# Score weights of both batches in the prologue, and U on eight array tiles

## What is computed

```python
q, k, v = heads(layernorm(x) @ Wq), heads(ctx @ Wk), heads(ctx @ Wv)
attn = softmax(q @ k.T / 8)                       # per head, over 77
x = x + tanh(g_xattn) * (merge(attn @ v) @ Wo + bo)
h = relu(fixed_quant(qlinear(layernorm(x), w1, b1)))
x = x + tanh(g_ffn) * qlinear(h, w2, b2)          # qlinear rounds input, weight and bias
```

## Time and profile before

| | us |
|---|---|
| median of 3 runs | 125.9 (125.42 to 126.14) |
| the profiled execution | 125.8 |
| its span, first to last instruction | 123.8 |
| busy: PE / PEld / DVE / ACT / POOL | 118.5 / 107.4 / 98.2 / 78.2 / 84.6 |

### The profile page before, as it was taken

The page is one execution under the profiler, slowest core; times in us unless marked ns, Lnnn a source line. Parts: engine busy times, 40 slices in busy tenths (PEclk is TensorE's granted clock), DMA queues, the critical chain, the costliest instruction groups (busy, mean ns, idle before and its releaser), DMA issues.

```text
span 123.8 us, 2908 instructions
## 1 busy us (share of the span) xinstructions
PE 118.5 (96%) x1029; PEld 107.4 (87%) x1029; DVE 98.2 (79%) x218; ACT 78.2 (63%) x167; POOL 84.6 (68%) x157
## 2 busy tenths in 40 slices
PE   7999999979999999999999999999999999999990
PEld 2689968969995999999999999999999997988780
DVE  3017999698999989989899999999797969447981
ACT  4155591999888484999384857566664728357520
POOL 3002229288794979698989958995899595987610
PEclk9999999999999999999999999999999999999999
DMA  2999699300000000000002000100200020020104
GB/s 68 338 266 334 227 380 382 139 5 0 3 0 8 0 0 3 0 0 5 0 0 85 5 0 36 48 5 3 83 1 0 5 87 0 0 80 10 54 30 169
DMA packets 5311, 8.86 MB, mean 72 GB/s; under 512 B 1175, under 2 KB 2226, under 8 KB 5170
## 3 DMA queue, kind: packets, MB, share of 16 engines
q1 hardware_dynamic: 5210, 8.61, 19.5%
q10 hardware_dynamic: 88, 0.08, 0.2%
HBM read 6.59 MB, written 2.10 MB: 70 GB/s over the span
## 4 chain that ended last, share of the span: by engine, by line
PE 86%; DVE 5%; ACT 3%; POOL 2%; issue 2%; DVEq 0%; POOLq 0%; ACTq 0%
PE sc_ps L741 21%; PE of_ps L774 20%; PE h_ps L801 9%; PE tr_ps L753 7%; PE of_ps L816 7%; PE tr_ps L686 4%; PE of_ps L679 3%; PE h_ps L708 3%; PE tr_ps L724 2%; PE h_ps L695 2%; PE tr_ps L816 1%; PE sc_ps L816 1%; POOL probs L266 1%; PE sc_ps L695 1%; PE of_ps L782 1%
## 5 line engine op out<-in xcount | busy, mean ns | idle before, releaser
L741 PE MATMUL sc_ps<-a_sb,xT 128*128 128x308 f32 x192 | 31.2, 311 | 0.0
L774 PE MATMUL of_ps<-u_sb,pT 128*128 128x256 f32 x240 | 30.6, 279 | 0.3 <-ACT x2T L414 0.2
L774 PEld LDWEIGHTS of_ps<-u_sb,pT 128*128 128x128 f32 x240 | 29.1, 188 | 1.2 <-issue 1.1
L741 PEld LDWEIGHTS sc_ps<-a_sb,xT 128*128 128x128 f32 x192 | 27.5, 189 | 0.7 <-issue 0.4
L382 ACT ACTIVATE probs<-probs,rstd 128x616 f32<-128x616 f32 x16 | 13.1, 817 | 23.1 <-DVE probs L543 23.0
L408 ACT ACTIVATE hid_q<-h_ps,b1z 128x256 int8<-128x256 f32 x58 | 24.8, 495 | 3.9 <-PE h_ps L801 3.9
L266 POOL TENSOR_TENSOR probs<-probs,rden 128x616 f32<-128x616 f32 x16 | 19.5, 1221 | 3.2 <-DVE rden L553 3.2
L311 POOL CAST hid<-hid_q 128x512 bf16<-128x512 int8 x27 | 15.8, 611 | 2.0 <-ACT hid_q L408 2.0
L801 PE MATMUL h_ps<-x2T,w1T 128*128 128x256 bf16 x128 | 16.6, 273 | 0.0
L538 DVE TENSOR_REDUCE mx<-sc_ps 128x8 f32<-128x616 f32 x16 | 12.7, 792 | 4.7 <-PE sc_ps L741 4.6
L394 ACT CAST pT<-tr_ps 128x640 fp32r<-128x640 f32 x16 | 11.1, 691 | 4.8 <-PE tr_ps L753 4.8
(11 more groups left out here) (103 smaller groups left out, 187.7 us busy)
## 6 DMA issues: line engine op xcount, KB each, us to landing
w_sb<-in_L_ffn_w_dram SPq DMA_DIRECT2D x2, 1024.0 KB, 10.9
out_dram<-x_sb SPq DMA_DIRECT2D x7, 256.0 KB, 2.5
x_sb<-in_x_dram SPq DMA_DIRECT2D x4, 256.0 KB, 8.6
x_sb<-in_x_dram SPq DMA_DIRECT2D x1, 1024.0 KB, 9.8
wk_sb<-in_L_xattn_Wk_dram SPq DMA_DIRECT2D x1, 512.0 KB, 3.8
wq_sb<-in_L_xattn_Wq_dram SPq DMA_DIRECT2D x1, 512.0 KB, 5.7
wv_sb<-in_L_xattn_Wv_dram SPq DMA_DIRECT2D x1, 512.0 KB, 8.3
wo_sb<-in_L_xattn_Wo_dram SPq DMA_DIRECT2D x1, 512.0 KB, 8.5
```

What stands on the lines that cost most here:

```text
L741: ins = nc.tensor.matmul(sc_ps[:, a, 0:HALF], xT[:, T % 2, p, c, :], a_sb[:, q, T // TB, c, HALF * a:HALF * a + HALF], start=first, stop=last)
L774: ins = nc.tensor.matmul(attn_ps, pT[:, T % 2, p, P * c:P * c + P], u_sb[:, q, MC * (T // TB) + c, :], start=first, stop=last)
```

## The change

A is made for both batches at once: each matmul has 154 columns (77 of each batch) in place of 77, in four units (c, half) that go to four pairs of PSUM banks, all in the prologue. ACT copies batch 0's part as the high part and batch 1's part whole to `a1_whole`; POOL makes batch 1's high part (a cast) and low part out of that (`a1_parts`, once ahead of `rstd_first(2, 4)`, once in step 0). The two ACT copies in each of steps 0 and 1 go.

U is made with the even heads' values on rows 0 to 63 and the odd heads' on rows 64 to 127. Each matmul takes 64 rows and 32 columns; even and odd windows alternate, and the tables EVEN and ODD put four windows of each parity in a round, so that a round has eight different tiles. The heads' order in the probabilities becomes even heads first. A window that straddles two head pairs takes two matmuls: 24 for a batch in place of 20. Batch 1's U moves from step 3 to step 2. Its first two low parts are made on POOL (steps 2 and 3), one in place of DVE. In the loop, DVE takes `denominators(1)` first in step 0 and ACT takes the exponentials of tile 1 first; in the prologue ACT takes `exponentials(0)` ahead of `xT_copy(2)`. The values go to `vz` in one copy of 128 rows in place of two of 64 each time.

```diff
+EVEN = ((0, 0), (1, 0), (2, 0), (3, 1)), ((4, 1), (5, 2), (2, 1), (7, 2)), ((8, 3), (9, 3), (6, 2), (7, 3))
+ODD = ((2, 0), (3, 1), (0, 0), (1, 0)), ((2, 1), (7, 2), (4, 1), (5, 2)), ((6, 2), (7, 3), (8, 3), (9, 3))
...
-        a_banks = {(0, 0): sc_ps[:, :, 0:HALF], (0, 1): of_ps[:, :, 0:HALF],
-                   (1, 0): h_ps[:, :, 0:HALF], (1, 1): h_ps[:, :, 0:HALF]}
-        def a_of(b, c, part):
-            return a_sb[:, part, b, c, :].rearrange("p (a m) -> p a m", a=2)
+        v_banks = of_ps[:, 1, 0:2 * MP], tr_ps[:, 0:2 * MP]
+        def values_psum(j):
+            return v_banks[j].rearrange("p (c b m) -> p c b m", c=2, b=B)
+        a_banks = {(0, 0): of_ps, (1, 0): sc_ps, (0, 1): tr_banks, (1, 1): h_ps}
+        def a_psum_of(c, half, b):
+            return a_banks[c, half][:, :, 0:2 * MP].rearrange("p q (j b m) -> p q j b m", j=2, b=B)[:, :, :, b, :]
+        def a_part(a, half):
+            return a.rearrange("p (q j m) -> p q j m", q=2, m=M)[:, :, 2 * half:2 * half + 2, :]
+        a_units = ((0, 0), (1, 0), (0, 1), (1, 1))
...
+            def a1_parts(c):
+                pool.wait_ge(a1_copied, 3 + c)
+                nc.gpsimd.tensor_copy(a_sb[:, 0, 1, c, :], a1_whole[:, c, :]).then_inc(a1_high, 1)
+                pool.wait_ge(a1_high, c + 1)
+                nc.gpsimd.tensor_tensor(a_sb[:, 1, 1, c, :], a1_whole[:, c, :], a_sb[:, 0, 1, c, :].bitcast(F32),
+                                        ALU.subtract).then_inc(a1_low, 1)
             def u_low(n):
-                pool.wait_ge(copied, 3)
-                nc.gpsimd.tensor_tensor(u_of(1, n, 1), full[:, 0:2 * D], u_of(1, n, 0).bitcast(F32),
-                                        ALU.subtract).then_inc(copied_low, 1)
+                pool.wait_ge(u_high, 4 + n)
+                pool.wait_ge(u1_copied, n + 1)
+                nc.gpsimd.tensor_tensor(u_of(1, n, 1), u1_whole[:, n, :], u_of(1, n, 0).bitcast(F32),
+                                        ALU.subtract).then_inc(u1_low, 1)
...
             rstd_first(0, 2)
+            a1_parts(0)
...
-                if s in (0, 1):
-                    a_low(s, s + 1)
+                if s == 0:
+                    a1_parts(1)
                 if s % 2 == 1 and 3 <= s < TILES - 4:
                     rstd_first(s + 3, s + 5)
-                if s == 3:
-                    u_low(1)
+                if s in (2, 3):
+                    u_low(s - 2)
...
-            a_copy(0, 0)
-            a_copy(0, 1)
+            a_copy(0)
+            a1_copy(0)
+            a_copy(1)
+            a1_copy(1)
+            a_copy(2)
+            a_copy(3)
             act.wait_ge(xT_psum, 2)
             nc.scalar.copy(xT[:, :, 0, :, :].rearrange("p i c n -> p i (c n)"),
-                           h_ps[:, 0, :].rearrange("p (i n) -> p i n", i=2)).then_inc(xT_high, 2)
+                           of_ps[:, 0, :].rearrange("p (i n) -> p i n", i=2)).then_inc(xT_high, 2)
+            a1_copy(2)
+            a1_copy(3)
             act.wait_ge(vz_zero, 1)
...
+            nc.scalar.copy(values_of(1), values_psum(1)).then_inc(v23_ready, 1)
+            exponentials(0)
             xT_copy(2)
-            exponentials(0)
             u_copy(0, 0)
             u_copy(0, 1)
             u_copy(0, 2)
...
             for s in range(TILES):
-                if s == 0:
-                    pT_copy(0)
-                    xT_copy(3)
                 if live(s + 1):
                     exponentials(s + 1)
-                if s > 0:
-                    pT_copy(s)
-                if live(s + 3) and s > 0:
+                pT_copy(s)
+                if live(s + 3):
                     xT_copy(s + 3)
                 if live(s + 4) and s > 0:
                     minus_centred(s + 4)
                 if s == 0:
-                    a_copy(1, 0)
-                    nc.scalar.copy(full[:, :].rearrange("p (a m) -> p a m", a=2), a_banks[1, 0]).then_inc(copied, 1)
                     round_weights(w1_in, w1_sb, w1q, w1_rounded)
                 if s == 1:
-                    a_copy(1, 1)
-                    act.wait_ge(copied_low, 1)
-                    nc.scalar.copy(full[:, :].rearrange("p (a m) -> p a m", a=2), a_banks[1, 1]).then_inc(copied, 1)
                     w1T_copy()
...
-                if s == 3:
-                    u_copy(1, 0)
-                    u_copy(1, 1)
-                    act.wait_ge(copied_low, 2)
-                    nc.scalar.copy(full[:, 0:2 * D], u_banks[1, 1]).then_inc(copied, 1)
-                    u_copy(1, 2)
...
                 if s == 2:
+                    for n in range(2):
+                        u_copy(1, n)
+                        u1_copy(n)
+                if s == 3:
+                    u_copy(1, 2)
                     round_weights(w2_in, w2_sb, w2q, w2_rounded)
...
-            a_low(0, 0)
-            a_low(0, 1)
+            for n in range(len(a_units)):
+                a_low(n)
...
-                if live(s + 1) and s > 0:
+                if live(s + 1):
                     denominators(s + 1)
                 probsT_low(s)
                 if live(s + 3):
                     rowsT_low(s + 3)
-                if s == 0:
-                    denominators(1)
-                if s in (3, 4):
-                    u_low(1, 2 * (s - 3))
+                if s == 4:
+                    u_low(1, 2)
...
-            def score_weights(b, c, pairs):
-                for j in pairs:
+            def score_weights(c, half):
+                for j in range(2 * half, 2 * half + 2):
                     for q in range(2):
-                        rows = slice(HD * q, HD * q + HD)
-                        ins = nc.tensor.matmul(a_banks[b, c][:, q, M * j:M * j + M], wqT[rows, j, P * c:P * c + P],
-                                               kT[rows, j, M * b:M * b + M], start=True, stop=True, tile_position=(HD * q, 0))
-                if PAIRS - 1 in pairs:
-                    ins.then_inc(a_psum, 1)
+                        rows, at = slice(HD * q, HD * q + HD), MP * (j % 2)
+                        ins = nc.tensor.matmul(a_banks[c, half][:, q, at:at + MP], wqT[rows, j, P * c:P * c + P],
+                                               kT[rows, j, :], start=True, stop=True, tile_position=(HD * q, 0))
+                ins.then_inc(a_psum, 1)
+            def output_window(b, q, w, j):
+                rows, at = slice(HD * q, HD * q + HD), FLANK + WIN * w - MW * j
+                chunk, row = (WINDOWS * q + w) // 4, WIN * ((WINDOWS * q + w) % 4)
+                bank, col = ((0, 0), (0, D), (2, 0), (1, 0), (1, D))[chunk]
+                two = w % 5 == 2
+                return nc.tensor.matmul(u_banks[b, bank][row:row + WIN, col:col + D], vz[rows, b, j, at:at + WIN],
+                                        wo_sb[rows, j, :], start=not two or j % 2 == 0, stop=not two or j % 2 == 1,
+                                        tile_position=(HD * q, row))
             def output_weights(b):
-                for g in range(HMP // WIN):
-                    j, col = g // (VW // WIN), WIN * (g % (VW // WIN))
-                    c, row = g // (P // WIN), WIN * (g % (P // WIN))
-                    if (b, j, col) == (0, 2, 0):
-                        pe.wait_ge(v23_ready, 2)
-                    dst = u_banks[b, c // 2][:, D * (c % 2):D * (c % 2) + D]
-                    ins = nc.tensor.matmul(dst[row:row + WIN, :], vz[:, b, j, col:col + WIN], wo_sb[:, j, :],
-                                           start=True, stop=True, tile_position=(0, row))
-                    if row + WIN == P and (c % 2 == 1 or c == MC - 1):
-                        ins.then_inc(u_psum, 1)
+                for r in range(3):
+                    if (b, r) == (0, 1):
+                        pe.wait_ge(v23_ready, 1)
+                    for i in range(4):
+                        even = output_window(b, 0, *EVEN[r][i])
+                        odd = output_window(b, 1, *ODD[r][i])
+                even.then_inc(u_psum, 1)
+                odd.then_inc(u_psum, 2)
...
-                    score_weights(0, c, (2 * j, 2 * j + 1))
+                    score_weights(c, j)
+            pe.wait_ge(a_ready, 1)
+            pe.wait_ge(a1_copied, 1)
             for T in range(2):
                 pe.wait_ge(xn_first, T + 1)
                 for c in range(DK):
-                    ins = nc.tensor.transpose(h_ps[:, 0, D * T + P * c:D * T + P * c + P], xn[:, T, P * c:P * c + P], ident[:, :])
+                    ins = nc.tensor.transpose(of_ps[:, 0, D * T + P * c:D * T + P * c + P], xn[:, T, P * c:P * c + P], ident[:, :])
                 ins.then_inc(xT_psum, 1)
             pe.wait_ge(wv_in, 16)
-            keysT(wv_sb, v_psum, (0, 1), 0)
-            pe.wait_ge(a_high, 2)
-            pe.wait_ge(a_ready, 1)
+            keysT(wv_sb, v_psum, (0, 1), v_banks[0])
+            pe.wait_ge(a_high, len(a_units))
+            pe.wait_ge(a_ready, 2)
+            pe.wait_ge(a1_copied, 2)
             scores(0)
```

(61 more changed lines are left out.)

53 lines of the change are left out of this document (25 added, 28 removed).

## The result

The changed kernel takes 123.75 us in the median of 4 runs (123.67 to 124.02), the kernel before 125.75 in the same set of 4 (125.42 to 126.14). The ratio is 0.9843, with a 95% interval of 0.9809 to 0.9877: faster by 1.6%, 2.0 us. The forecast was 123.3 with a range of 122.5 to 124.9, so 2.0 us came where 2.5 were foreseen. The profiled execution takes 123.75 us with a span of 122.0; before it was 125.8 with 123.8. The work around the span differs by 0.2 us between the two.

A forecast was written before the change was run, and what follows sets the result against it. PE was taken to bound the kernel, busy 96% of the span, except up to scores(2); 1.95 by scores(3) plus 0.86 for batch 1's U, less 0.3 for a wait, gave 2.5 us: 125.8 to 123.3, range 122.5 to 124.9.

The forecast's parts named there:

- Score weights: Prologue and loop: two blocks of 1.05 us removed, 2.10 us; 154-column pairs at 0.131 us add 0.31 us.
- U: Each batch's U block: eight tiles at a time, 6 passes, 1.44 us instead of 2.30, 0.86 saved.
- (a): Rival for U: only four tiles run together, 12 passes, +1.3 us each, 124.9 us; chance 0.11.
- (d): Rival for U: alternating tiles leave only pairs, 24 passes, +3.9 us each, 129.9 us; chance 0.05.
- Up to `scores(2)`: Start of the loop: 1.6 us less PE work gives nothing, two waits of some 0.85; start 21.7 against 21.66.
- Step 0 and 1: PE itself is late next: probsT(1) at 25.5, 0.9 gained; scores(3) at 26.6 to 26.65, 1.95 gained.
- The cast on POOL: The 616-column cast in a1_parts on POOL, taken as 0.75 us, with 0.4 to 1.5 as ends.
- 0.2 us of cover: Step 2: softmax_scale(2) ends at 30.1 on POOL, PE arrives at 30.35; a cast of 1.5 would cost 0.5.
- Up to `scores(5)`: Loop sum before the step 5 wait: 1.95 by scores(3) plus 0.86 for batch 1's U, 2.8 us.
- less 0 to 0.6 for the wait of step 5, for which I take 0.3: Near 46 us: PE waits for POOL's probs(5), 0.6 likeliest, 0 to 1 as bounds; 0.3 taken in the sum.
- (b): Rival: chains of the start weigh more, slow POOL cast or softmax-bound step 0; 0.5 + 0.5, 124.3 us; chance 0.10.
- (c): Rival: PE bound everywhere, no wait in the loop, gain 4.3 us at most, 122.3 us; chance 0.07.

The follow-up runs named there:

- e5: The changed kernel measured again, nothing altered: 123.60 us, ratio 0.984 to the kernel before.
- e11: Changed kernel with center(1) ahead of one u_low on DVE, x2T copies of steps 3, 4 earlier on ACT, GpSimd's u_low(1) in step 5: 123.88 us.
- e12: Changed kernel with center(1) ahead of u_low(0,1) on DVE in the prologue, measured on a second occasion: 123.33 us, ratio 0.9813.
- e7: Changed kernel with center(1) moved ahead of u_low(0,1) on DVE in the prologue: 123.26 us, ratio 0.9805.
- e9: Changed kernel with the order of ACT and DVE in prologue and step 0 put back to that of before: 124.03 us, ratio 0.985.
- e3: Changed kernel with the old U (four tiles at a time, 10 passes), all else as changed: 124.49 us, ratio 0.9908.
- e6: Changed kernel with the x2T copies of steps 3 and 4 moved earlier on ACT, right behind xT_copy: 123.81 us, ratio 0.9836.
- e8: Changed kernel with center(1) ahead of one u_low on DVE and x2T copies of steps 3 and 4 earlier on ACT: 123.30 us, ratio 0.9806.
- e10: Kernel before with the new U alone, and in step 3 the x2T copy ahead of U's four copies on ACT: 124.78 us, ratio 0.9927.

## Why the prediction was right, and where it was wrong

- **Score weights: right.** A pair of 154-column halves takes 0.131 us as taken from the earlier trace rows, the two blocks of 1.05 are gone, and from the first score-weight matmul to `scores(0)` it is 3.78 us instead of 3.49: + 0.29 against the 0.31 of the sum. In e5, e11 and e12 it is 4.0 to 4.1: there `x` landed later against the weights, and TensorE waits 0.14 to 0.26 us for DVE's first low part, which the new prologue puts ahead of the first rows' transposes.
- **U: right.** Six passes of 0.216 and 1.46 us a block against 1.44 forecast. Rivals (a) and (d) fall with it. The next pass's weight loads take no time of their own here either (0.216 us a pass), so the trace again disagrees with the rule of the Trainium skill ("TensorE: Matmul & The Clock Gate", Part 3, The mechanism) that the prediction left out.
- **Up to `scores(2)`: right.** TensorE is held for 0.90 and 0.87 us by `probs(0)` and `center(1)` (0.73 and 0.72 in the brackets) against "some 0.85" each, and a start at 21.54 (21.73 with the 0.19 of earlier loads added) against 21.7. e7 shows the cause: take the low part out from ahead of `center(1)`, and 0.6 us come.
- **Step 0 and 1: the time right, its reason in part wrong.** `probsT(1)` at 25.30 and `scores(3)` at 26.26, with the 0.19 added 25.49 and 26.45, against 25.5 and 26.6; no wait for `probs(1)`. But the working gave this to the new order on ACT and DVE, and e9 has `probsT(1)` at 25.32 without it, 0.3 earlier counted from `scores(0)`. `scores(3)` is 2.13 us earlier without the 0.19, against 1.95 in the sum. I followed how early the new order makes `probs(1)` and didn't work out how late the old order would make it with the blocks gone.
- **The cast on POOL: right, the cover behind it not.** The cast takes 0.70 us against 0.75 by length:

```profile
12.77 0.70 POOL L301 CAST a_sb<-a_whole 128x616 fp32r<-128x616 f32 x1 [1.75 <-ACT a_whole L418]
```

  But softmax(2), for which the working saw "0.2 us of cover", was late by 0.17 us: it ends at 30.13 (30.32 with the 0.19, against 30.1), and TensorE, ready at 30.02 (30.21 against 30.35), was there first. That is the prediction's own sign that "the working is wrong there even if the total fits": TensorE waits for POOL in step 2.
- **Up to `scores(5)`: the sum fits by luck in part.** It is 2.97 earlier, 2.78 without the loads' 0.19, against 2.8. Of the two terms the 1.95 by `scores(3)` came out at 2.13 and the 0.86 for U(1) at 0.65: from `probsT` to `scores` a step with U takes 2.98 us before and 2.19 now, 0.79 less, and the hold at `probsT(2)` takes 0.17 of it. The two misses cancel.

- **Steps 3 and 4: the step that failed.** The term "less 0 to 0.6 for the wait of step 5, for which I take 0.3" was mis-sized and misplaced. Measured is 0.24 at `attend(3)` and 0.55 at `attend(4)`, 0.8 together, for a copy on ACT. The sentence "DVE's lag of up to 0.6 reaches no wait of PE's" is the wrong one: it does reach one, by way of ACT. `center(4)` is late on DVE, the exponentials wait for it, and all of ACT's queue with the x2T copy at its end waits with them. How much of this is DVE's lag is not separated: at `attend(3)` the late start of `exp(4)` alone is 0.31 us, and in e3, where `exp(4)` is not late, `attend(3)` comes 1.78 us after `scores(5)` as in the late steps and waits for nothing (it is 2.20 in the changed kernel), while `attend(4)` waits there as well. The forecast wait for `probs(5)` did not show, since the earlier one had already taken up the time; with the earlier one shortened (e6, e8) it came, 0.33 us. The first of the two hid the second.
- **Late steps: small, unforeseen.** They take 6.03 us on average from `scores(8)` to `scores(14)` instead of 5.99, 0.23 us in all by `scores(15)` (last section).
- Of the rivals (b) had the right kind of mechanism, chains of the start that weigh more, and the time fell between it and the forecast. Of the places it names, the cover at step 2 did fall short, by 0.17; most of the loss lay elsewhere, with ACT in steps 3 and 4. (c) did not come: TensorE was not bound everywhere.
- Two slips in the prediction's sums change nothing: DVE's 4.30 and 3.96 make 8.26, not 8.24, and half of 1.7 off the 123.3 is 122.45, not 122.3 in (c).

The sum by the traces: 2.78 - 0.79 - 0.08 - 0.23 = 1.68 us, and 1.87 with the 0.19 of the loads, where the span shrank by 1.85; the medians say 2.0, with an interval of 1.5 to 2.4.

## What to carry to other kernels

A saving on the bound engine is a saving only as far as the next queue in which something it needs stands behind something nobody needs yet; look at each engine's order around the step, not only at its busy share, and put the copy that frees the busiest engine's buffer first (worth 0.4 to 0.6 us in e10, though nothing in e6's medians, where the next wait stood close behind). Follow lateness through engines: DVE's lag reached TensorE by way of ACT, though no wait of TensorE's for DVE stood in that stretch. Where two waits follow each other, the earlier one hides the later one, so removing one wait is worth less than its length (0.88 us became 0.3 in e6); and moving work off one engine's tight step puts it ahead of another's (e11).
